# Seven places in the order of work of a four-layer kernel: first turns, bias rows, first logits, passages between layers, masked units, last tiles

## The chip, the cores and the metric

One NeuronCore of a Trainium2 chip runs the whole program. The metric is the time of one execution on the device, in microseconds (us). The engines are named as in the profile: PE (TensorE), DVE (VectorE), ACT (ScalarE), POOL (GpSimd) and SP (SyncE, whose queue issues the DMA transfers). They run their own lists of instructions and meet at semaphores only.

## The reference

The input is x, 2 x 512 tokens of 256 numbers (fp32), eight tiles of 128 tokens. Four layers follow one another, each of the form

```
xn = layernorm(x);  x = x + attn(xn) * silu(ffn(xn))
```

- Layer 0: attention with 16 heads of 128, in which the probabilities are summed over the queries and multiply the values; a mixture of eight experts (256 to 1024 to 256, gelu, a low-rank side path, two experts to a token, 160 slots each) plus a shared expert of the same size.
- Layer 1: an RWKV step (key, value, receptance, and one recurrent state that enters at the first token only); a linear layer.
- Layer 2: attention across the heads' first positions with rotary factors, and eight dense experts (256 to 256) weighted by a gate.
- Layer 3: differential causal attention, 8 heads; a feed-forward network (1024 hidden) with a Walsh-Hadamard transform of the hidden rows.

## The kernel before

Everything stays in on-chip memory; weights are fetched ahead of each stage. Almost every matrix product is made as three products of rounded halves (`product`, lines 101 to 103): an operand is split into a rounded part (ACT or DVE writes it) and the rest (DVE or POOL subtracts). So each stage has the rhythm: PE fills a bank of PSUM, ACT copies it rounded, DVE writes the rest, PE reads both.

Each engine's list is written out by hand, so the order of the statements below is the order of the work.

- **Start.** DVE and POOL normalise the eight tiles of x (`statistics`, `rsqrt`, `normalised`, line 1345), four tiles (batch 0) first. PE turns a tile with `turn_xn` (line 804), ACT copies it (`turned`, line 1941), DVE writes the rest (`turned_rest`, line 1352). Then PE projects head 0: batch 0's first two products, the turns of tiles 4 to 7, then the rest. POOL meanwhile runs `split_qkv(1, ...)` (lines 649 and 652), which splits head 1's weights, and behind it `rest_k(0, ...)` (line 658), the key rests that head 0's scores wait for.
- **Heads.** Sixteen heads, each with eight scores, eight maxima (DVE, line 1394), eight exponentials (ACT, line 1963) and eight accumulations. Head 15 also makes the router's logits: `logits_rows` after score 2, `logits_turn` (line 830) after score 5, which waits for ACT's copy of the logits (line 1972).
- **Experts.** Eight rounds. In a round PE makes nine hidden tiles (`hidden`; tile n needs the bank of tile n - 4 free, which is when DVE has split it, line 1547), turns back the rows of the expert before (`rows_back`), turns the next slots and makes the second product (`rows_of`, which reads split f + 1 for its step f). DVE runs `expert`: for each n a rounding (line 1541) and a rest (line 1547); before n == 2 it runs `rows_biased` (lines 1529 and 1532), which adds the bias to the rows of the expert before. SP stores those rows, loads the bias (line 476), and then, in its next turn, the next slots (lines 486, 487) and the next weights (line 467, 1060 KB). ACT begins to round those weights (line 2023) beside the next expert's hidden tile 0.
- **Shared expert.** `shared_hidden` and `shared_rows` on PE, gelu on ACT (line 2104), `shared_split` on DVE (lines 1580 to 1589). `combine(b)` (line 1611) joins the two experts' rows of a batch; it is called for batch 1 after the residuals of batch 0.
- **Passage from layer 0 to 1.** After the last tile of `shared_rows(1)` PE turns tiles 0 to 3 of the new xn, waits for their rests and projects.
- **Layer 1.** Projections of batch 0 (`rwkv_product`), turns of tiles 4 to 7, four products with a Hadamard matrix (`hadamard`, line 1121) for layer 3's down weights, a wait for ACT's four copies of them (line 2158), projections of batch 1, then `lin_rows` and `out_rows`. DVE: `first_key`, `mixed_values`, `wkv`, then `residuals(1, b)`. ACT: `keys1`, `exponentials1`, `receptance`, then the rounding of layer 2's weights (line 2165), from which POOL subtracts (line 748).
- **Layer 3.** 24 units (g, h, k) of attention: scores, an exponential (line 2301), and, if the unit lies on the diagonal, a mask by POOL (line 791); PE multiplies a unit's probabilities two units later (`values3`, line 1268). Half of the groups have two units, the one off the diagonal first. Then the down product, and `token_major` (line 1070), the output product, with two tiles to a bank; DVE multiplies and adds by pairs (`residual`, lines 1326 and 1329), and SP stores by pairs (line 575).

## Time and profile before

| | |
|---|---|
| median of 3 runs | 888.36 us (887.53 to 889.39) |
| the profiled execution | 889.76 us, of which its span is 888.0 |
| PE busy | 851.4 us (96%) |
| DVE busy | 630.2 us (71%) |
| ACT busy | 465.1 us (52%) |
| POOL busy | 451.2 us (51%) |
| PE's mean granted clock | 0.996 |

Engines work side by side, so busy times don't add up to the span. A granted clock of 1.00 is 2.4 GHz, 0.50 is 1.2 GHz. In a timeline row the first number is the start from the span's beginning, the second the duration; a bracket at its end is the idle time before it and the instruction whose end released it. Products that follow one another overlap in the rows, so the distance of two starts is what one costs. Rows of SPq are the issuing of a transfer, not the transfer.

### The profile page before, as it was taken

How to read it: one execution, taken by the hardware profiler on the slowest of the kernel's cores; microseconds unless marked ns; L12 is line 12 of the kernel's file. 1: busy time of each engine (PE TensorE's matmuls, PEld its weight loads, DVE VectorE, ACT ScalarE, POOL GpSimd, SP SyncE). 2: the span in 40 equal slices, each digit the busy share in tenths (PEclk: the TensorE clock that was granted, in tenths of full speed). 3: DMA queues.
4: the chain of work that ended last, by engine and by line, in shares of the span. 5: the costliest groups of instructions: out<-in, count | busy, mean ns of one | idle time of the engine just before them, and what ended most of it. 6: DMA issues, size and time to landing. Idle time of an engine off the chain costs nothing.

```text
span 888.0 us, 15400 instructions
## 1 busy us (share of the span) xinstructions
PE 851.4 (96%) x5344; PEld 708.8 (80%) x5344; DVE 630.2 (71%) x1255; ACT 465.1 (52%) x928; POOL 451.2 (51%) x299
## 2 busy tenths in 40 slices
PE   5999999999999999999999999899999999989998
PEld 4888888888856899999999878678788887866677
DVE  7798989898987756645656867576677575348655
ACT  2666666666654566655642384633343343256632
POOL 5576767676624555665655003069626227426620
PEclk9999999999999999999999999999999999999999
DMA  8101010101007276465113050011110010000001
GB/s 324 37 19 35 18 35 18 35 18 36 0 0 264 84 256 200 148 205 178 53 35 122 3 201 1 1 49 48 35 59 24 1 60 1 1 1 2 3 1 48
DMA packets 22142, 59.02 MB, mean 66 GB/s; under 512 B 2896, under 2 KB 13392, under 8 KB 19024
## 3 DMA queue, kind: packets, MB, share of 16 engines
q1 hardware_dynamic: 20560, 54.20, 18.4%
q0 software_dynamic: 1536, 4.20, 1.4%
q8 instruction: 30, 0.49, 0.2%
q14 instruction: 16, 0.13, 0.0%
HBM read 50.00 MB, written 8.39 MB: 66 GB/s over the span
## 4 chain that ended last, share of the span: by engine, by line
PE 85%; DVE 7%; ACT 4%; issue 2%; DMA 1%; POOL 1%; POOLq 0%; SPq 0%; DVEq 0%; ACTq 0%
PE banks L101 25%; PE banks L102 24%; PE banks L103 24%; PE banks L1268 3%; PE banks L1255 2%; PE banks L1070 2%; PE banks L940 1%; DVE banks L1784 1%; DVE arenaB_rounded L1541 1%; DMA arenaD<-in_wexp 1%; DVE arenaC_rounded L1547 1%; PE banks L1110 1%; PE banks L875 1%; PE banks L876 1%; DVE arenaC_rounded L1793 1%
## 5 line engine op out<-in xcount | busy, mean ns | idle before, releaser
L1963 ACT ACTIVATE banks<-banks,small 128x512 f32<-128x512 f32 x128 | 84.9, 663 | 79.7 <-DVE small L1394 79.7
L1394 DVE TENSOR_REDUCE small<-banks 128x1 f32<-128x512 f32 x128 | 86.8, 678 | 10.5 <-PE banks L103 10.5
L101 PE MATMUL banks<-xnT_rounded,arenaD_rounded 128*128 128x512 f32 x224 | 90.8, 405 | 2.9 <-DVE s_tok_rounded L1352 2.9
L102 PE MATMUL banks<-s_tok_rounded,arenaD_rounded 128*128 128x512 f32 x224 | 91.3, 408 | 0.0
L103 PE MATMUL banks<-arenaC_rounded,arenaD_rounded 128*128 128x512 f32 (+1 forms) x256 | 89.6, 350 | 0.0
L103 PE MATMUL banks<-xnT_rounded,arenaC_rounded 128*128 128x512 f32 x192 | 77.5, 403 | 0.0
L103 PE MATMUL banks<-xnT_rounded,arenaD_rounded 128*128 128x512 f32 x192 | 75.9, 395 | 0.0
L101 PE MATMUL banks<-arenaC_rounded 128*128 128x512 f32 (+1 forms) x192 | 71.3, 371 | 2.8 <-DVE arenaC_rounded L1547 2.8
L1409 DVE SCALAR_TENSOR_TENSOR arenaC<-banks,small,arenaC 128x512 f32<-128x512 f32 x96 | 71.2, 741 | 0.0
L102 PE MATMUL banks<-arenaD_rounded,arenaC_rounded 128*128 128x512 f32 (+1 forms) x192 | 68.5, 357 | 0.0
L663 POOL TENSOR_TENSOR arenaD_rounded<-arenaC,ones 128x512 fp32r<-128x512 f32 x30 | 31.3, 1042 | 55.1 <-DVE arenaC L1409 54.1
L101 PE MATMUL banks<-arenaB_rounded,arenaC_rounded 128*128 128x320 f32 (+2 forms) x176 | 57.4, 326 | 0.0
L101 PE MATMUL banks<-xnT_rounded,arenaB_rounded 128*128 128x512 f32 x128 | 52.0, 406 | 3.3 <-DVE arenaC_rounded L1793 1.1
L101 PEld LDWEIGHTS banks<-xnT_rounded,arenaD_rounded 128*128 128x128 f32 x224 | 43.4, 194 | 13.9 <-POOL arenaC_rounded L677 1.9
L103 PEld LDWEIGHTS banks<-arenaC_rounded,arenaD_rounded 128*128 128x128 f32 x256 | 48.0, 188 | 5.5
L102 PEld LDWEIGHTS banks<-s_tok_rounded,arenaD_rounded 128*128 128x128 f32 x224 | 43.3, 193 | 9.9
L709 POOL TENSOR_TENSOR arenaD_rounded<-arenaD,arenaB_rounded 128x1024 fp32r<-128x1024 f32 (+1 forms) x12 | 37.5, 3140 | 26.8 <-ACT arenaB_rounded L2023 26.8
L658 POOL TENSOR_TENSOR arenaD_rounded<-arenaD,arenaC_rounded 128x512 fp32r<-128x512 f32 x32 | 41.4, 1294 | 17.8 <-ACT arenaD L1954 17.8
L2209 ACT ACTIVATE arenaC<-banks 128x512 f32<-128x512 f32 x32 | 18.9, 599 | 59.5 <-PE banks L103 59.5
L1784 DVE TENSOR_TENSOR banks<-banks,arenaC 128x512 f32<-128x512 f32 x32 | 22.4, 700 | 36.7 <-PE banks L103 32.3
L103 PE MATMUL banks<-arenaB_rounded,arenaC_rounded 128*128 128x256 f32 (+1 forms) x144 | 47.7, 331 | 0.0
L102 PE MATMUL banks<-arenaB_rounded,arenaC_rounded 128*128 128x320 f32 (+2 forms) x144 | 47.3, 329 | 0.0
(408 smaller groups left out, 2634.5 us busy)
## 6 DMA issues: line engine op xcount, KB each, us to landing
arenaD<-in_wexp SPq DMA_DIRECT2D x8, 1060.0 KB, 6.6
arenaD<-in_wexp SPq DMA_DIRECT2D x8, 1024.0 KB, 4.9
arenaC<-in_wqkv SPq DMA_DIRECT2D x16, 384.0 KB, 3.1
arenaD<-in_wexp SPq DMA_DIRECT2D x8, 512.0 KB, 3.6
slots<-arenaB SPq DMA_DIRECT2D x1, 2560.0 KB, 10.3
arenaB<-in_sw SPq DMA_DIRECT2D x1, 2084.0 KB, 7.4
arenaC<-in_wo SPq DMA_DIRECT2D x1, 2048.0 KB, 14.9
arenaC<-slots SPq DMA_DIRECT2D x8, 256.0 KB, 2.8
```

The costliest lines, as they stand in the source:

```text
L101: pe.matmul(o, r(lhs[0]), r(rhs[0]), start=start, stop=False)
L102: pe.matmul(o, r(lhs[0]), r(rhs[1]), start=False, stop=False)
L103: return pe.matmul(o, r(lhs[1]), r(rhs[0]), start=False, stop=stop)
L658: pool.tensor_tensor(r(klo[q][:, sl]), klo[q][:, sl], rounded(kT[q][:, sl]), ALU.subtract).then_inc(klo_done, 1)
L663: pool.tensor_tensor(r(acc_hi[b]), acc[b], ones[:, 0:1].to_broadcast([P, S]), ALU.mult).then_inc(acc_rounded, 1)
L709: pool.tensor_tensor(r(v), v, rounded(h), ALU.subtract).then_inc(w_split, 1)
L1268: mm = pe.matmul(bank[6 + m % 2][32 * hh:32 * hh + 32, 256 * which + q0 - 256 * h:256 * which + 256], lhs, prob3[u % 4][:, hh, at:at + w], ...
L1394: dve.tensor_reduce(negmax[:, n % 4:n % 4 + 1], bank[3 + n % 4][:, :], AX.X, ALU.max, negate=True).then_inc(max_done, 1)
L1409: ins = dve.scalar_tensor_tensor(acc[n // ST], prob[n % 4], inv, acc[n // ST], ALU.mult, ALU.add)
L1784: dve.tensor_tensor(v, v, gs[n % 2], ALU.mult).then_inc(gu_done, 1)
L1963: act.activation(prob[r], prob[r], ACT.Exp, bias=negmax[:, r:r + 1], accum_out=rowsum[:, r:r + 1]).then_inc(exp_done, 1)
L2209: act.activation(gs[n % 2], bank[n % 2][:, :], ACT.Silu).then_inc(silu2_done, 1)
```

## The change

Seven places; nothing is computed otherwise.

1. First turns: PE runs twelve products of a matrix of ones into an unused bank before its first turns; POOL waits for all eight normalised tiles before it splits head 1's weights.
2. First logits: `logits_turn` is called after score 7 and not after score 5.
3. Expert bias rows: `rows_biased` is called before hidden tile 6 and not before tile 2.
4. Passage from layer 0 to 1: tiles 0 to 3 are turned ahead of the last tile of `shared_rows(1)`; the eight operations of `combine(1)` go in between the steps of `shared_split(1, ...)`.
5. Layer 1 and the passage to layer 2: two of the four Hadamard products and their copies move behind the turns of layer 2's tiles 4 to 7; ACT rounds layer 2's weights before `keys1(1)` and not after `receptance(1)`; tiles 0 to 3 are turned ahead of the last tile of `out_rows`.
6. Masked units first: a group's unit on the diagonal comes before the one off it.
7. Last tiles: the last two tiles are multiplied, added and stored one by one, the last from a bank of its own.

```diff
-        UNITS3 = [(g, h, k) for g in range(8) for h in range(2) for k in range(0, 2 * h + 2, 2)]
+        UNITS3 = [(g, h, k) for g in range(8) for h in range(2) for k in range(2 * h, -2, -2)]
         DIAGONAL3 = [n for n, (g, h, k) in enumerate(UNITS3) if k == 2 * h]
...
+        WARM_UP = 12
...
-            for i in range(NT // 2):
+            for i in range(NT // 2 - 1):
                 sp.wait_ge(x_done, (layers - 1) * NT // 2 + i + 1)
                 sp.dma_start(out[256 * i:256 * i + 256, :].rearrange("(n p) d -> p n d", p=P), x[:, 2 * i:2 * i + 2, :]).then_inc(x_out, 16)
-            sp.wait_ge(x_out, 16 * NT // 2)
+            for t in (NT - 2, NT - 1):
+                sp.wait_ge(x_done, layers * NT // 2 + t - NT + 2)
+                sp.dma_start(out[P * t:P * t + P, :], x[:, t, :]).then_inc(x_out, 16)
+            sp.wait_ge(x_out, 16 * (NT // 2 + 1))
...
             rsqrt(0, (2, 3))
+            pool.wait_ge(xn_done, NT)
             split_qkv(1, 1, 0)
             rest_k(0, 0, 0)
             rest_k(0, 0, 1)
...
+            pe.wait_ge(filled, ONES)
+            for n in range(WARM_UP):
+                pe.matmul(bank[7][:, 0:P], ones[:, :], ones[:, :], start=True, stop=True)
             turn_xn(0, range(NT // 2))
...
                     if last and n == 2:
                         pe.wait_ge(v_done, 2 * NH)
                         logits_rows()
-                    if last and n == 5:
-                        logits_turn()
                     if n == 7:
+                        if last:
+                            logits_turn()
                         colsum(h, 0, whole=last)
...
             def shared_rows(b):
                 for t in range(ST * b, ST * b + ST):
+                    if t == NT - 1 and layers > 1:
+                        turn_xn(1, range(ST))
                     o = bank[4 + t // 2][:, (t % 2) * D:(t % 2 + 1) * D]
...
-                def hadamard():
-
-                    pe.wait_ge(wff3_in, 16)
-                    pe.wait_ge(kr_done, 2)
-                    for i in range(4):
-                        if i >= 2:
-                            pe.wait_ge(had_copied, i - 1)
-                        pe.matmul(bank[i % 2][:, :], con[:, C_HAD:C_HAD + P], w_down3[:, 2 * i:2 * i + 2, :].rearrange("p f d -> p (f d)"),
+                HAD_BANK = (0, 1, 6, 7)
+
+                def hadamard(parts):
+
+                    for i in parts:
+                        pe.matmul(bank[HAD_BANK[i]][:, :], con[:, C_HAD:C_HAD + P], w_down3[:, 2 * i:2 * i + 2, :].rearrange("p f d -> p (f d)"),
                                   start=True, stop=True).then_inc(had_ready, 1)
 
-                turn_xn(1, range(ST))
                 pe.wait_ge(fold_split, 7)
                 turned(1, 1)
                 rwkv_product(0, 0, (0, 1))
...
                 turn_xn(1, range(ST, NT))
                 if layers > 2:
-                    hadamard()
-                    pe.wait_ge(had_copied, 4)
+                    pe.wait_ge(wff3_in, 16)
+                    pe.wait_ge(kr_done, 2)
+                    hadamard((0, 1))
+                    pe.wait_ge(had_copied, 2)
                 turned(1, 3)
                 pe.wait_ge(kr_done, 2)
                 rwkv_product(0, 1, (0, 1))
...
                 pe.wait_ge(rwkv_done, 2)
                 for t in range(ST, NT):
+                    if t == NT - 1 and layers > 2:
+                        turn_xn(2, range(ST))
                     out_rows(t)
                 if layers > 2:
-                    turn_xn(2, range(ST))
                     pe.wait_ge(wq_split, 1)
                     qkv_rows(w_qkv2, w_qkv2_hi, 2, range(ST))
             if layers > 2:
 
                 turn_xn(2, range(ST, NT))
+                hadamard((2, 3))
                 qkv_rows(w_qkv2, w_qkv2_hi, 2, range(ST, NT))
+                pe.wait_ge(had_copied, 4)
                 pe.wait_ge(qkv_done, 2 * NT)
...
@@ -1267,7 +1279,7 @@
                             lhs = ones[:, 0:32] if which else v3[:, ST * b + kt, 32 * head:32 * head + 32]
                             mm = pe.matmul(bank[6 + m % 2][32 * hh:32 * hh + 32, 256 * which + q0 - 256 * h:256 * which + 256],
                                            lhs, prob3[u % 4][:, hh, at:at + w],
-                                           start=(kt == 0), stop=(kt == 2 * h + 1), tile_position=(0, 32 * hh))
+                                           start=(kt == 2 * h), stop=(kt == 1), tile_position=(0, 32 * hh))
                     return mm
...
-                    if k == 0 and m >= 2:
+                    if u == GROUPS3[m][0] and m >= 2:
                         pe.wait_ge(norm3_done, m - 1)
                     mix3(m, u, 0)
...
                 pe.wait_ge(wgo3_in, 32)
                 pe.wait_ge(norm3_done, 16)
-                token_major(yT3, w_out3, 4, s_ready)
+                token_major(yT3, w_out3, 4, s_ready, range(NT - 1))
+                pe.wait_ge(ffn_done, NT)
+                for c in range(DC):
+                    mm = pe.matmul(bank[3][:, 0:D], yT3[:, c, (NT - 1) * P:NT * P], w_out3[:, c, :], start=(c == 0), stop=(c == DC - 1))
+                mm.then_inc(s_ready, 1)
...
             def expert(e, q, back=None, last=False):
                 for n in range(NF + 2):
 
-                    if n == 2 and back is not None:
+                    if n == 6 and back is not None:
                         rows_biased(*back)
                     if n <= NF:
                         dve.wait_ge(hid_done, HID0 + 9 * e + n + 1)
@@ -1602,15 +1618,17 @@
...
-            def combine(b):
-
-                dve.wait_ge(rows_got[b], 16 * 2 * ST)
-                dve.wait_ge(bias_done, 3)
-                for k in range(2):
-                    for t in range(ST * b, ST * b + ST):
-                        ins = dve.scalar_tensor_tensor(got[0][:, t, :], got[k][:, t, :], wt[:, t, k:k + 1], got[0][:, t, :] if k else sb2,
-                                                       ALU.mult, ALU.add)
-                    link(ins)
+            def combine(b, parts=range(2 * ST)):
+
+                for j in parts:
+                    if j == 0:
+                        dve.wait_ge(rows_got[b], 16 * 2 * ST)
+                        dve.wait_ge(bias_done, 3)
+                    k, t = j // ST, ST * b + j % ST
+                    ins = dve.scalar_tensor_tensor(got[0][:, t, :], got[k][:, t, :], wt[:, t, k:k + 1], got[0][:, t, :] if k else sb2,
+                                                   ALU.mult, ALU.add)
+                    if j % ST == ST - 1:
+                        link(ins)
...
             combine(0)
             shared_sum(0)
             shared_sum(1)
-            shared_split(1, range(2, NF + 1))
+            for f, parts in zip(range(2, NF + 1), ((), (0, 1), (2, 3), (4,), (5,), (6,), (7,))):
+                shared_split(1, (f,))
+                combine(1, parts)
...
             residuals(0, 0)
-            combine(1)
             rests(1, 0)
             shared_sum(2)
             shared_sum(3)
...
-                between(3)
+                for i in range(NT // 2 - 1):
+                    residual(3, i)
+                dve.wait_ge(silu_done, NT // 2 * 4)
+                for t, o in ((NT - 2, bank[7][:, 0:D]), (NT - 1, bank[3][:, 0:D])):
+                    dve.wait_ge(s_ready, NT * 3 + t + 1)
+                    g = g_tok[:, t, :]
+                    link(dve.scalar_tensor_tensor(g, o, 1.0 - LAMBDA_INIT, g, ALU.mult, ALU.mult))
+                    dve.tensor_tensor(x[:, t, :], x[:, t, :], g, ALU.add).then_inc(x_done, 1)
...
@@ -2152,17 +2178,21 @@
                 keys1(0)
                 exponentials1(0)
                 turned(1, (2, 3))
+
+                def hadamard_copy(i, b0):
+                    act.wait_ge(had_ready, i + 1)
+                    act.copy(had_b[:, 2 * i:2 * i + 2, :].rearrange("p f d -> p (f d)"), bank[b0][:, :]).then_inc(had_copied, 1)
+
                 if layers > 2:
-                    for i in range(4):
-                        act.wait_ge(had_ready, i + 1)
-                        act.copy(had_b[:, 2 * i:2 * i + 2, :].rearrange("p f d -> p (f d)"), bank[i % 2][:, :]).then_inc(had_copied, 1)
+                    hadamard_copy(0, 0)
+                    hadamard_copy(1, 1)
                 receptance(0)
+                if layers > 2:
+                    act.wait_ge(w2_in, 16)
+                    act.copy(r(part(arenaC, 10752, DC * (768 + E2))), part(arenaC, 0, DC * (768 + E2))).then_inc(wq_rounded, 1)
                 keys1(1)
                 exponentials1(1)
                 receptance(1)
-                if layers > 2:
-                    act.wait_ge(w2_in, 16)
-                    act.copy(r(part(arenaC, 10752, DC * (768 + E2))), part(arenaC, 0, DC * (768 + E2))).then_inc(wq_rounded, 1)
                 gate_silu(1)
                 turned(2, (0, 1))
...
                 round_gateup(0, 0, 0)
                 qkv_copy(2, 2, 4)
                 turned(2, (2, 3))
+                hadamard_copy(2, 6)
+                hadamard_copy(3, 7)
                 round_gateup(1, 1, 0)
                 qkv_copy(2, 4, 6)
                 round_down(0, 0, 0)
```

## Rows read from the trace of the kernel before

**Rows 1.** The page, chain that ended last, share of the span by engine.

```profile
PE 85%; DVE 7%; ACT 4%; issue 2%; DMA 1%; POOL 1%; POOLq 0%; SPq 0%; DVEq 0%; ACTq 0%
```

**Rows 2.** PE's waits, whole span: us in total, times, longest.

```profile
PE banks L101 <- DVE s_tok_rounded L1352: 7.1, 5, 1.7
PE banks L804 <- DVE xn L1345: 7.0, 2, 6.5
PE banks L101 <- DVE arenaC_rounded L1547: 5.2, 8, 1.1
...
PE banks L830 <- ACT arenaC L1972: 1.8, 1, 1.8
PE banks L1268 <- POOL arenaB L791: 1.5, 1, 1.5
```

**Rows 3.** Timeline, 6 to 19 us: start, duration, engine and line.

```profile
6.94 0.73 DVE L1345 TENSOR_SCALAR xn<-x,meanvar,rstd 128x256 f32<-128x256 f32 x2 [0.27 <-POOL rstd L593]
...
12.99 1.46 POOL L649 TENSOR_TENSOR arenaD_rounded<-arenaC,ones 128x768 fp32r<-128x768 f32 x1
...
13.06 3.44 DVE L1345 TENSOR_SCALAR xn<-x,meanvar,rstd 128x256 f32<-128x256 f32 x2 [0.27 <-POOL rstd L593]
...
18.39 0.66 PE L101 MATMUL banks<-xnT_rounded,arenaD_rounded 128*128 128x512 f32 x1 [1.40 <-DVE s_tok_rounded L1352]
```

**Rows 4.** Stretches of 1 us: busy time (x instructions) by engine, granted clock, DMA.

```profile
14.00:15.00 1.00, 1.00 (x4) 0.81 (x3) 1.00 (x2) 0.00 (x0) 0.92 (x2) 1.00 1.09 471
...
19.00:20.00 1.00, 1.00 (x4) 0.81 (x3) 0.03 (x1) 0.27 (x1) 0.65 (x1) 0.50 1.11 475
...
22.00:23.00 1.00, 1.00 (x6) 0.81 (x5) 0.85 (x4) 0.00 (x0) 0.00 (x0) 1.00 0.00 0
```

**Rows 5.** Timeline, PE, the four Hadamard products.

```profile
517.78 3.68 PE L1121 MATMUL banks<-arenaD,con 128*128 128x512 f32 x8
```

**Rows 6.** Timeline, DVE, last head's seventh row maximum.

```profile
260.23 0.69 DVE L1394 TENSOR_REDUCE small<-banks 128x1 f32<-128x512 f32 x1
```

**Rows 7.** Timeline, one round of the expert loop (DVE, PE, SP queue, ACT).

```profile
334.25 0.69 DVE L1529 TENSOR_TENSOR arenaC<-banks,arenaD 128x512 f32<-128x512 f32 x1
334.97 0.43 DVE L1532 TENSOR_TENSOR arenaC<-banks,arenaD 64x256 f32<-64x256 f32 x1
...
336.50 0.41 PE L101 MATMUL banks<-arenaC_rounded,arenaB_rounded 128*128 128x320 f32 x1 [0.67 <-DVE arenaC_rounded L1547]
...
336.96 0.40 SPq L476 DMA_DIRECT2D arenaD<-in_b  x1
...
342.18 0.33 SPq L467 DMA_DIRECT2D arenaD<-in_wexp  x1
...
349.55 0.61 ACT L2023 CAST arenaB_rounded<-arenaD 128x512 fp32r<-128x512 f32 x1
```

**Rows 8.** DMA issues of the expert weights: the loop's six, then the slowest.

```profile
arenaD<-in_wexp SPq DMA_DIRECT2D x6, 1060.0 KB, 6.6
...
arenaD<-in_wexp SPq DMA_DIRECT2D x1, 1060.0 KB, 7.5
```

**Rows 9.** Timeline around the end of layer 0 (PE, DVE).

```profile
492.02 0.43 DVE L1580 CAST arenaC_rounded<-arenaB 128x512 fp32r<-128x512 f32 x1 [0.38 <-ACT arenaB L2104]
...
496.74 0.39 PE L1051 MATMUL banks<-xn_rounded,arenaB_rounded 128*128 128x256 f32 x1
...
503.55 1.67 DVE L1611 SCALAR_TENSOR_TENSOR arenaC<-arenaC,small,arenaB 128x256 f32<-128x256 f32 x4
```

**Rows 10.** Timeline around layer 1 (PE, POOL, DVE).

```profile
522.14 0.50 PE L101 MATMUL banks<-xnT_rounded,arenaC_rounded 128*128 128x512 f32 x1 [0.68 <-ACT arenaB L2158]
...
533.79 4.06 POOL L748 TENSOR_TENSOR arenaC_rounded<-arenaC,arenaC_rounded 128x1552 fp32r<-128x1552 f32 x1 [17.35 <-ACT arenaC_rounded L2165]
...
536.63 1.77 DVE L1329 TENSOR_TENSOR x<-x,g_tok 128x512 f32<-128x512 f32 x1
```

**Rows 11.** Timeline, DVE, the last pair of tiles.

```profile
883.99 0.69 DVE L1326 SCALAR_TENSOR_TENSOR g_tok<-banks,g_tok 128x512 f32<-128x512 f32 x1 [0.31 <-PE banks L1070]
```

## Prediction

> **What bounds the kernel now.** I read the chain of work that ended last first: TensorE (PE) holds 85% of it, VectorE (DVE) 7%, ScalarE (ACT) 4% [rows 1]. So an edit is worth what it takes out of PE's idle time or slow clock, and nothing else. The second view is PE's own waits: 7.1 us in five stalls for the rests of the turned activations, 7.0 us for the normalised rows (6.5 of it the kernel's start), 5.2 us in eight stalls in the experts, 1.8 us for the logits, 1.5 us for the last causal mask, and others of 2.0 us or less that no edit names [rows 2]. The third is the order of time around each edit, the fourth the granted clock.
>
> The profiled execution took 889.76 us, 1.76 outside its span of 888.0; the runs' median is 888.36. I take the gain off the profiled one and carry it to the median.
>
> **First turns.** POOL's work on head 1's weights begins at 12.99, and beside it two normalisations of the tokens take 3.44 us, where the same pair alone took 0.73 [rows 3]. The new wait holds that work (the 1.46 us rounding and the subtraction behind it) until the eighth tile. The pair then ends at 13.79 and not 16.50: 2.7 us. The held work, 3.3 us long, ends near 17.2; its readers are head 1's first projection (after 21) and, behind it in POOL's queue, head 0's first key rest, which started at 19.35. Both are later, so the wait costs nothing. From the end of the pair to the first projection of batch 1 ran 18.39 - 16.50 = 1.9 us [rows 3]: it would start at 15.7.
>
> That needs PE free by 13.8. It is not at today's pace: the twelve projections from 10.01 start four to the microsecond until 14.84 [rows 4]. At 1.2 GHz (granted 0.50) four start, at 2.4 GHz six in one with overlap: 0.43 against 0.235 us each [rows 4]. The twelve warm-up products are 128 columns of fp32. Four of 512 columns took 3.68 us [rows 5], so one of 128 costs 0.22 at 2.4 GHz and 0.44 at 1.2: 2.6 to 5.3 us. PE stands idle for the first 6.5 us [rows 2] and its companions start work at 1.6, so they end about when the first turn may start; at worst 0.4 after, which the turns' own wait for rows hides. Today the dense stretch from 18.39 brings the clock from 0.50 back to 1.00 by 22 [rows 4]; the warm-up is as dense, so I expect the fast pace at 10.0. The twelve projections are then through at 12.9, and batch 1's 24 run at 0.235, where today eight ran at 0.43 (19 to 22 [rows 4]): 1.5 us more. All together 4.1. But by 19 it was at 0.50, after PE had mostly waited from 16 to 18.4, and the new order keeps gaps of some 1.5 us before 10.0 and before 15.7. If the warm-up bought nothing, the twelve end at 14.85, the turns at 16, batch 1 starts at 17.8: 0.6. Bounds 0.6 and 4.1; I take 3.4, near the top, because more work lies ahead of both gaps than today.
>
> The Trainium skill, "TensorE: Matmul & The Clock Gate", section "What's actually happening", says that the number of slow products at a kernel's start varies between executions of the same kernel. By it this term would come in some runs and not in others, 4.1 or down to 0.6; the trace of one execution can't show that.
>
> **First logits.** The eight small turns move from after score 5 to after score 7. PE's 1.8 us wait [rows 2] goes, but scores 6 and 7 need banks that DVE frees, and DVE's maximum of score 6 at 260.23 [rows 6] has no wait in front: it was DVE that came late, not the score. Head 15's end is DVE and ACT in turn. Worth 0.1; bounds 0 and 0.3. Their reader, at 267, is not touched.
>
> **Expert bias rows.** Two additions, 0.69 and 0.43 us, sit on DVE before hidden tile 2's rounding, and PE then waits 0.67 for the split of tile 1 [rows 7]. Without them it ends 0.8 earlier, ahead of the 335.83 at which PE wants it. At tile 6 they lie behind split 4, the last that a hidden tile waits for; splits 5 to 8 come 1.1 us later (split 8 near 342.3), and the second product reads split 8 at 343.1. The first of the eight stalls (1.1) has no bias rows before it: 5.2 - 1.1 = 4.1 over seven.
> What becomes late is SP. It waits for the additions before it stores the rows and loads the bias, and behind these stand the next slots and the next 1060 KB. The additions end near 339.3; today the bias load goes out 1.56 us after they end (335.40 to 336.96 [rows 7]), and two slot loads and the branch put another 1.7 before the big one: near 342.6 instead of 342.18 [rows 7]. It lands after 6.6 us as the median of six, 7.5 at the worst [rows 8]: 349.2 to 350.1. ACT rounds from it at 349.55 [rows 7], in the new order 0.67 earlier, at 348.9. Late by 0.3 to 1.2, of which the round soaks up 0.45: today 1.12 us of additions cost PE only 0.67. I take 0.1 a round, 3.5, since half of the six land sooner than that median. Bounds 1.0 (0.5 a round) and 4.1.
>
> **Passage 0 to 1.** Today PE waits 1.7 after the four turns, the longest of the five stalls [rows 2]. The turns now stand before the last shared tile, whose 2.9 us cover copy and rest. But the second combination moves into the split loop: eight operations of 0.42 us, 3.3 in all, between splits with 0.38 us of idle time in front of each [rows 9], so DVE leaves the loop 1.25 us later (five such gaps of about 0.4 are all it can use). The matmul at 496.74 already waits for the last split (it shows 0.39 us, its like 0.28 [rows 9]) and passes on 0.85 of it; the normalised rows come 1.25 later, so the turns end at 505.1 and the last tile at 508.05. Gain 0.4; bounds 0 and 1.7.
>
> **Passage 1 to 2.** Of the four Hadamard products (3.68 us [rows 5]) two move behind the later turn, into one of the five stalls; with them goes the 0.68 us wait for the last copy [rows 10]. PE reaches the next projections at about 519.95, not 522.14 [rows 10]: 2.2 with the 0.4. Then the chain through DVE decides. The rounding of the next layer's weights moves before the second batch's keys: ACT ends it near 524.0 and POOL subtracts for 4.06 us [rows 10], 524 to 528.1. In that stretch DVE does the first key's small steps and batch 0's products, all with both inputs in SBUF. The nearest row is an addition of that kind, which took 1.77 for 0.69 and ended 0.5 after POOL's subtraction, begun at 533.79 [rows 10]. So the first key waits to 528.1, exponentials and gates follow it, and batch 0's residual starts near 535.9, where it is today. What is left is the 1.08 that the residual no longer loses to POOL: rows normalised 1.0 earlier. The turn put before the last output tile hides 1.2 of PE's next wait. PE starts the projections near 544.0 instead of 546.18; the two Hadamard products behind the next turn (1.75 against a stall of 1.4) give back 0.2. For both passages together 2.0; bounds 0.4 (only the first) and 3.1 (DVE not held up).
>
> The Trainium skill, "SBUF — State Buffer", section "Who interferes with whom", speaks against this move: a DVE instruction with two SBUF inputs is shut out for the whole of a GpSimd instruction that reads SBUF. By it the small steps wait out all of the 4.06 us and the sum is my 2.0; without it, 2.7.
>
> **Masked units first.** PE's last wait is 1.5 us for the mask of the very last unit [rows 2], with 0.1 more before it. Now the last unit has no mask, and its neighbours' mask ends under the last scores. Inside the loop two masks still follow each other, and PE has no gap. 1.6; bounds 0.8 and 1.9.
>
> **Last tiles.** The last pair's product starts on DVE at 883.99, after 0.31 us of waiting, takes 0.69 [rows 11], and an addition as long follows: 885.4. In the new order tile 6 can't start before the third residual ends, at 883.7, and four half-size operations of 0.42 [rows 9] with the waits between them take 1.75: 885.4 again. Only the last store is half as large. 0.1; bounds 0 and 0.6 (half of the last pair's two operations).
>
> **Sum.** 3.4 + 0.1 + 3.5 + 2.0 + 1.6 + 0.1 = 10.7 us. 889.76 - 10.7 = 879.1 profiled, 888.36 - 10.7 = 877.7 as median. All upper bounds (4.1, 0.3, 4.1, 3.1, 1.9, 0.6) make 14.1: 874.3. All lower ones (0.6, 0, 1.0, 0.4, 0.8, 0) 2.8: 885.6.
>
> **Rivals.**
> The clock does not hold: the fast pace is lost in a gap and the first term is 0.6, the sum 7.9: 880.5. For it: the clock fell once in this stretch. Against: PE is idle for less of it now. 0.20.
> The expert loads become the bound: landings of 7 us and more together with the stores give 0.5 a round: 880.2. For it: the median landing is already at the limit. Against: the 0.45 of slack. 0.13.
> A passage gives nothing: DVE's backlog of combinations or POOL's subtraction reaches PE, 2.0 becomes 0.4: 879.3. 0.12.
> Slower: SP's queue in the experts. If each of six loads came 2.0 us later than I place it, the loop would lose what all else gains: (10.7 + 1.8) / 6 = 2.1 a round decides for slower by over 0.2%. It needs landings over 9 us. 0.04.
> No change: the gains lie on PE but some other engine holds the same pace, within 1.8 us of 888.36. The 851 us for which PE was busy speak against it. 0.04.
> The forecast: 0.47.
>
> **Numbers.** 0.2% (1.8 us) is what a measurement of this kernel tells from no change. All cases but the last two are faster: 0.92; 0.04 within; 0.04 slower. For 8 in 10 I go from 874.3 to 883.0: above it lie half of the cases in which two rivals meet, no change and slower.
>
> **What would show it.** Right: the pair of normalisations near 0.8 us; six products a microsecond from 10; no wait on split rows in experts 1 to 7; PE's projections of layer 2 two microseconds sooner after the experts; no wait for a mask at the end. Wrong: granted clock 0.50 between 15 and 20; ACT idle before the first rounding of a round for a DMA; DVE's first-key steps of 0.16 us stretched to over 2 with PE waiting behind them; a wait on the last output tile's turn of over 2 us.

## The result

The changed kernel takes 882.98 us (median of 5 runs, 880.82 to 883.76) against 888.36 for the kernel before, a ratio of 0.9923 with an interval of 0.9908 to 0.9939. That is faster by 5.4 us, half of the 10.7 forecast, and inside the predicted range (874.3 to 883.0) by 0.02 us only: 877.7 was forecast. The profiled executions stand at 889.76 and 883.27, 6.5 us apart; the table below goes by them. Each entry is what PE gains in us between two marks that both kernels have; the times are those of the changed kernel. (The same product of the last head starts at 250.00 before and at 245.45 after, so 4.55 us are gained by then.)

| stretch | forecast | trace |
|---|---|---|
| start to the last head (245.45) | 3.4 | 4.55 |
| to the first expert's stall (313.31) | 0.1 | 0.09 |
| experts (to 445.94) | 3.5 | 1.49 |
| offset products and shared expert (to 489.35) | 0 | -1.62 |
| both passages (to 549.66) | 2.0 | 3.16 |
| layer 2 and the start of layer 3 (to 780.73) | 0 | -0.08 |
| attention of layer 3 (to 847.55) | 1.6 | -1.49 |
| end | 0.1 | 0.43 |
| sum | 10.7 | 6.53 |

The first turns, the passages and the end came out higher than forecast, the experts and the attention lower, and one loss stands where no edit is. The waits of PE in the changed kernel, beside those of before [rows 2]:

```profile
PE banks L101 <- DVE arenaC_rounded L1563: 3.2, 5, 1.1
PE banks L1267 <- ACT arenaC L2333: 2.4, 5, 0.9
PE banks L101 <- DVE s_tok_rounded L1368: 1.4, 1, 1.4
PE banks L809 <- DVE xn L1361: 1.3, 3, 0.8
```

The three s_tok stalls between the layers are gone (1.72, 1.05 and 1.46 us before), and so is the wait for the last mask; of the two at the start one is left, and the other stands under POOL's subtraction now (1.6 us). The experts' stalls fell from eight to five and not to one. The second row, which counts one of the two buffers only, holds a wait for an exponential that comes back in the loop of layer 3's attention.

**Start** (timeline of DVE, POOL and PE, beside [rows 3]; then two windows beside [rows 4], whose columns are the same):

```profile
12.77 0.74 DVE L1361 TENSOR_SCALAR xn<-x,meanvar,rstd 128x256 f32<-128x256 f32 x2 [0.26 <-POOL rstd L597]
13.58 1.47 POOL L653 TENSOR_TENSOR arenaD_rounded<-arenaC,ones 128x768 fp32r<-128x768 f32 x1 [0.85 <-DVE xn L1361]
15.40 0.50 PE L101 MATMUL banks<-xnT_rounded,arenaD_rounded 128*128 128x512 f32 x1 [1.40 <-DVE s_tok_rounded L1368]
```
```profile
17.00:18.00 1.00, 1.00 (x6) 0.82 (x5) 0.27 (x1) 0.60 (x1) 1.00 (x1) 1.00 0.84 360
19.00:20.00 1.00, 1.00 (x6) 0.81 (x5) 0.00 (x0) 0.68 (x3) 0.35 (x1) 1.00 0.96 410
```

The pair of normalisations took 0.74 us where it took 3.44. Batch 1's projections start 3.0 us earlier, six to the microsecond from the first, and that pace brings the other 1.55 of the 4.55.

**Experts** (timeline of the SP queue, ACT and PE, the round of [rows 7]; the DMA issues beside [rows 8]):

```profile
336.31 0.40 SPq L477 DMA_DIRECT2D arenaD<-in_b  x1
338.52 0.33 SPq L468 DMA_DIRECT2D arenaD<-in_wexp  x1
```
```profile
339.94 2.19 ACT L2049 CAST arenaC_rounded<-arenaD 128x512 fp32r<-128x512 f32 x4 [3.82 <-DMA arenaD<-in_b]
345.45 0.62 ACT L2049 CAST arenaB_rounded<-arenaD 128x512 fp32r<-128x512 f32 x1 [1.22 <-DMA arenaD<-in_wexp]
```
```profile
347.57 0.41 PE L101 MATMUL banks<-arenaC_rounded 128*128 128x320 f32 x1 [0.50 <-DVE arenaC_rounded L1563]
...
arenaD<-in_wexp SPq DMA_DIRECT2D x6, 1060.0 KB, 7.1
```

Read it from the bottom. PE waits 0.50 for the split of tile 1. ACT hands out tile 1 only after its first rounding, and this waited 1.22 for the 1060 KB load. That load went out at 338.52, behind the stores and the bias load, and took 6.9. Before, it went out at 342.18; with the 4.63 us gained so far, 338.52 stands for 343.15, so it is 1.0 late in its round. In every round in which ACT waits for this load PE stalls two microseconds later (347.57, 365.13, 382.64, 416.99, by 0.48 to 0.58; by the distance to before's products each costs 0.64 to 0.74); in the other two it doesn't. ACT's wait of 3.8 for the bias load is another thing that the prediction did not see: the second group of roundings counts the bias load too.

**Clock after the experts and in layer 3's attention** (windows):

```profile
448.00:449.00 1.00, 1.00 (x7) 1.00 (x8) 0.00 (x0) 0.00 (x0) 0.00 (x0) 0.57 0.00 0
451.00:452.00 1.00, 1.00 (x4) 0.74 (x3) 0.90 (x5) 0.00 (x0) 0.00 (x0) 0.50 0.00 0
455.00:456.00 1.00, 1.00 (x6) 0.82 (x5) 0.00 (x0) 0.62 (x2) 0.75 (x1) 1.00 0.00 0
783.00:784.00 1.00, 1.00 (x16) 0.78 (x11) 0.00 (x0) 0.21 (x1) 0.72 (x1) 0.50 0.00 0
788.00:789.00 1.00, 1.00 (x20) 0.74 (x16) 1.00 (x1) 1.00 (x2) 0.17 (x1) 0.50 0.00 0
```

The kernel before fell to 0.50 (1.2 GHz) from 455.5 to 458.9, the changed one from 448.1 to 455.0. The offset products lost 0.35 by that (2.95 against 2.60 us), the turns of the last rows 0.6 (1.2 against 0.6), the first products of the shared expert 0.7: the 1.6 of the table. In the attention the kernel before kept 1.00 throughout; the changed kernel was at 0.50 from 782.6 to 789.5.

**The loop of layer 3's attention** (timeline of PE: before, then the changed kernel):

```profile
803.01 0.94 PE L1255 MATMUL banks<-g_tok,s_tok 32*128 32x256 f32 x16
...
799.35 0.94 PE L1267 MATMUL banks<-g_tok,s_tok 32*128 32x256 f32 x16 [0.20 <-ACT arenaB L2333]
```

The scores of a unit follow without a gap before, and wait 0.20 us for an exponential in the changed kernel. That wait comes once in every three units, six times in all.

**Passage 1 to 2** (timeline of POOL, DVE and PE, beside [rows 10]):

```profile
515.42 0.50 PE L101 MATMUL banks<-xnT_rounded,arenaC_rounded 128*128 128x512 f32 x1 [0.68 <-ACT arenaB L2184]
...
519.47 3.55 POOL L753 TENSOR_TENSOR arenaC_rounded<-arenaC,arenaC_rounded 128x1552 fp32r<-128x1552 f32 x1 [7.96 <-ACT arenaC_rounded L2192]
...
520.90 2.13 DVE L1740 TENSOR_TENSOR small<-small 128x2 f32<-128x2 f32 x1 [4.18 <-ACT small L2160]
...
538.62 0.47 PE L101 MATMUL banks<-arenaC_rounded,xnT_rounded 128*128 128x512 f32 x1
```

A step of two columns that takes 0.16 us took 2.13 and ended with POOL's subtraction. The wait of 0.68 for the last Hadamard copy is still there, behind two copies as behind four.

### The profile page after: what moved, and what is told of

Its sections match the earlier page's. It is cut to its first block, busy times and chain, and to the rows that moved or that the text cites. A ratio compares the mean times of both kernels' runs of the same rounds, so it can differ in the third digit from the quotient of the medians.

```text
span 881.4 us, 15452 instructions
## 1 busy us (share of the span) xinstructions
PE 857.4 (97%) x5368; PEld 712.3 (81%) x5368; DVE 625.3 (71%) x1257; ACT 465.3 (53%) x928; POOL 448.9 (51%) x299
## 4 chain that ended last, share of the span: by engine, by line
PE 83%; DVE 6%; DMA 4%; ACT 3%; issue 2%; SPq 1%; POOL 0%; DVEq 0%; ACTq 0%; POOLq 0%
PE banks L101 23%; PE banks L102 22%; PE banks L103 22%; PE banks L1280 4%; DMA arenaD<-in_wexp 3%; PE banks L1267 3%; PE banks L1080 1%; DVE banks L1803 1%; PE banks L948 1%; PE banks L1120 1%; PE banks L883 1%; PE banks L884 1%; DVE arenaC_rounded L1812 1%; PE banks L809 1%; DMA arenaC<-in_wqkv 1%
## 5 line engine op out<-in xcount | busy, mean ns | idle before, releaser
L101 PE MATMUL banks<-arenaB_rounded,arenaC_rounded 128*128 128x320 f32 (+2 forms) x176 | 57.4, 326 | 0.0
L597 POOL TENSOR_TENSOR rstd<-veps,mhalf 128x2 f32<-128x2 f32 x16 | 12.2, 761 | 72.7 <-DVE veps L1356 72.7
```

Of the source, the lines that this page charges most:

```text
L101: pe.matmul(o, r(lhs[0]), r(rhs[0]), start=start, stop=False)
```

## The experiments

Each kernel ran in 5 rounds against the kernel before on its own chip. The median of before was 890.04 us for the first four, 891.68 for the next four and 890.61 for the last four, so kernels are compared by their ratio to it. 0.001 of ratio is 0.9 us.

### Units in the old order: units_back

```
-UNITS3 = [... for k in range(2 * h, -2, -2)]
+UNITS3 = [... for k in range(0, 2 * h + 2, 2)]
```

The blocks that open and close a group's accumulation go back with it.

> The kernel after, with the units of layer 3's attention back in the old order (unmasked first). The changed kernel's trace has a wait of 0.20 us for an exponential once in each group and a period of 7.81 us a group where before had 7.60; it also has 6.9 us at granted clock 0.50 at the start of this attention. Theory A (the order itself costs 0.2 us a group, and its gain at the end, 1.5 us, only pays that back; the slow clock there is chance): the period is 7.60 again, PE waits 1.5 us for the last mask again, and the time is that of the changed kernel within 1 us, 881 to 883. Theory B (the new order also brings the clock down at the start): the clock stays at 1.00 there in this kernel and it is 1.5 us faster than the changed kernel. Theory C (the new order is worth the 1.6 us of the forecast): 1.5 us slower than the changed kernel, with the period unchanged.

0.9912 (0.9889 to 0.9935). The attention (from its first scores' start to the end of its last products) took 66.24 us, with the old wait of 1.49 at its end and no wait in the loop, and the clock fell at 784 here too. Theory B falls: the fall comes with the old order as well. A holds, C doesn't.

### Bias rows back: bias_back

```
-if n == 6 and back is not None:
+if n == 2 and back is not None:
```

> The kernel after, with the bias rows of the experts back at hidden tile 2. The changed kernel still has four stalls of 0.5 us for the split of tile 1, each behind a wait of ScalarE of 1.2 us for the next expert's first load. Theory A (the loads, issued 1.0 us later in their round than before, took most of this part's gain): seven stalls of 0.57 to 0.67 us come back, none of them with a wait for a load, and the kernel is slower than the changed one by 1.5 us only. Theory B (the forecast, 0.5 us a round): slower by 3.5 us.

0.9901 (0.9884 to 0.9918), no slower than the changed kernel. Seven stalls of 0.57 to 0.60 came back, and no ACT wait for a load. From the first rank product of the rows (the one that closes each half of an expert's second product) to the last it took 125.1 us, as before did, and the changed kernel 123.6. The same stretch, with the bias rows of the change, took 122.4 to 124.4 in no_warm, units_end and fill, and 125.1 to 127.7 in round_back, units_back and no_hold, where one load came so late that PE stalled for 1.8 to 2.7 us; in units_back and no_hold the clock fell behind it. The median of the seven traces is 124.4. So this part is worth about 0.7 us, in some executions nothing. The trace is A's (seven stalls, no wait for a load); that the whole runs aren't slower, neither theory had.

### Loads ahead of the stores: loads_first, stores_late

```
 for e in range(NE - 2):
     sp.wait_ge(hid_done, HID0 + 9 * e + 9)
     load_slots(e + 2, e % 2)
     load_first(e + 2, e % 2)
+    if e:
+        store_rows(e - 1, 1 - e % 2)
+        load_bias(e + 1, 1 - e % 2)
     sp.wait_ge(y_ready, 4 * e + 2)
     load_second(e + 2, e % 2)
-    store_rows(e, q)
-    load_bias(e + 2, q)
...
```

That is loads_first; in stores_late the added lines stand behind load_second. In both, two more things change: the loop is written out instead of run as a loop, and the bias load counts on the semaphore of the stores, so that ACT's second roundings don't wait for it. No run takes the three apart.

> The kernel after, with the DMA queue's order in the experts changed: the next slots and the first 1060 KB go out before the rows are stored and the bias is loaded, and the bias load is counted by another semaphore, so that ScalarE's second group of roundings doesn't wait for it. Theory A (the late first load causes the four stalls): the load goes out 2 us or more earlier, ScalarE doesn't wait for it, no stall is left but the first, and the kernel is 2 us faster than the changed one. Theory B (the stalls come from DVE's own queue of splits): ScalarE's wait goes, the stalls of 0.5 us stay, and the time is that of the changed kernel.

0.9864 (0.9839 to 0.9888), some 5 us faster than the changed kernel. The stretch accounts for 1.0 of it: it fell to 122.6 us. This execution also had no fall of the clock behind the experts and a shorter one in the attention, but one at the start. Two stalls were left besides the first, 0.54 and 0.93, each behind an ACT wait for the first load, which now landed after 8.4 us as the median.

> The kernel after, with the DMA queue's order in the experts changed once more: slots and first load, then the second load of the same expert, and only behind it the stores of the rows and the bias load, which is counted by another semaphore. With the loads ahead of the stores the first load went out earlier but took 8.4 us as its median instead of 7.1, and two of six rounds still stalled. Theory A (the stores and the bias load beside the first load lengthen it): the first load lands after 6.6 us or less as the median, ScalarE doesn't wait for it, no round but the first stalls, the stretch from the first rank product of the rows to the last takes 121.5 to 122.5 us (changed kernel 123.6, before 125.1), and the kernel is 2 us faster than the changed one. Theory B (the length of the landing has to do with something else, such as the slots): still 7 us and more, stalls in some rounds, stretch 122.7 or longer.

0.9860 (0.9833 to 0.9886). The stretch took 120.3 us, less than A expected, and the waits hold one stall in place of five. That is 3.3 us less than in the changed kernel; the whole runs are some 5.6 faster, and what the rest is no trace shows. SP queue, then PE's waits:

```profile
336.34 0.43 SPq L468 DMA_DIRECT2D arenaD<-in_wexp  x1
...
343.73 0.43 SPq L520 DMA_DIRECT2D rows<-arenaC  x1
```
```profile
PE banks L101 <- DVE arenaC_rounded L1564: 1.1, 1, 1.1
```

The load goes out 2.2 us sooner, lands after 6.9 as the median (the trace has the landing of three of the six), and ACT waits for none. 125.1 - 120.3 = 4.8 us: the bias rows' whole gain, 4.1 by the forecast's upper bound, was there, and the queue of loads had withheld it. Before had no ACT wait for a load, so its stalls were the bias rows'; the new queue with the bias rows at their old place was not run.

### Single-column products among the last rows: offs_spread

```
-rows_of(NE - 1, NE // 2 - 1, 1)
+rows_of(NE - 1, NE // 2 - 1, 1, offset_products)
```

In the second half of these rows, offset_products puts two of the twelve products behind each hidden tile's product from the second on; the block of twelve behind the rows is gone.

> The kernel after, with the twelve offset products of one column (24 passes in 3.1 us) moved from behind the last expert to places between the products of its last rows. In both traces the granted clock falls to 0.50 some 2 to 3 us after these begin, and stays there 3.4 us before and 6.5 us after. Theory A (the sparse stretch brings the clock down): the clock stays at 1.00 after the experts; PE waits 0.8 us for the copy of the last rows, which the products hid, and 2 to 3 us are gained all the same against the changed kernel. Theory B (the fall is due to the long dense stretch before, or to chance): the fall comes all the same, and the kernel is 0 to 0.5 us slower or faster.

0.9908 (0.9892 to 0.9923). The clock stayed at 1.00 after the experts. But it did so too in units_back, loads_first and no_warm, with the products at the old place. From the last rank product but one to the shared expert's first product it took 7.86 us (with 0.58 of waiting for the copy), against 7.02 in units_back and 7.94 in the changed kernel, whose clock had fallen and whose next products lost 0.7 more: the move costs 0.8 where the clock holds. The stretch of the experts, which holds the moved products here, took 129.0 us with a stall of 2.17 and a fall of the clock behind it. Open: whether the sparse stretch brings the fall.

### Masked first only at the end: units_end

```
-for k in range(2 * h, -2, -2)
+for k in ((2, 0) if g == 7 and h else range(0, 2 * h + 2, 2))
```

The accumulation's opening and closing blocks follow.

> The kernel after, with the masked unit first only in the very last of the sixteen groups of layer 3's attention, and unmasked first in all others. Theory A (0.2 us a group is the price of the order in the loop, 1.5 us its gain in the last group alone): the period is 7.60 us, no wait for an exponential in the loop, no wait for the last mask, and the kernel is 1.2 to 1.4 us faster than the changed one. Theory B (the two belong together): the wait at the end stays in some form, and the kernel is no faster than the one with all units back, within 0.5 us.

0.9902 (0.9875 to 0.9929). No wait at the end, none in the loop but at its start: A, as a structure. The clock was at 0.50 from 784 to 791, and the attention took 65.55 us with it, 1.3 less than the changed kernel.

### Filler behind the first scores: fill

```
 scores3(u)
+if u < 2:
+    for i in range(4):
+        pe.matmul(bank[7][:, 0:P], ones[:, :], ones[:, :], start=True, stop=True)
```

> The kernel after, with four more products of 128 columns, whose result nobody reads, behind each of the first two scores of layer 3's attention, where PE waits 0.9 us for an exponential. The changed kernel, the one with its units back and two others all show granted clock 0.50 for 3 to 7 us from there; before shows none. Theory A (the pauses of 0.9 us bring the clock down): it stays at 1.00 there, and the kernel is 1.5 us faster than the changed one. Theory B (the fall comes from something else, such as the small products of a quarter of the rows): the clock falls all the same, and the kernel is the same within 0.5 us or slower by what the products delay the scores.

0.9902 (0.9874 to 0.9931). The clock stayed at 1.00 and the attention took 65.0 us (changed kernel 66.9). The run's own time doesn't show this apart from noise.

### No warm-up: no_warm

```
-for n in range(WARM_UP):
-    pe.matmul(bank[7][:, 0:P], ones[:, :], ones[:, :], start=True, stop=True)
```

> The kernel after, without the twelve warm-up products at the start. Theory A (they set the pace of the first projections): the granted clock is 0.50 from 10 to 15 us, four products a microsecond, batch 1's projections start near 16.9 instead of 15.4, at 0.50 for 3 us more, and all that follows is 3 us later: 3 us slower than the changed kernel. Theory B (the wait of POOL gave most of the 4.6 us): 1 us slower or less.

0.9921 (0.9895 to 0.9946): as fast as the changed kernel, where A had 3 us slower. The profiled execution shows no fall of the clock behind its start, and its six runs had a mean granted clock of 0.998, the changed kernel's 0.994. Start (PE, timeline; windows):

```profile
18.09 0.50 PE L101 MATMUL banks<-xnT_rounded,arenaD_rounded 128*128 128x512 f32 x1 [1.56 <-DVE s_tok_rounded L1365]
```
```profile
13.00:14.00 1.00, 1.00 (x4) 0.80 (x3) 0.73 (x3) 0.00 (x0) 0.23 (x1) 1.00 0.95 410
19.00:20.00 1.00, 1.00 (x6) 0.81 (x5) 0.00 (x0) 0.20 (x1) 1.00 (x1) 1.00 0.99 426
```

Batch 1 started 2.7 us later than in the changed kernel, at 18.09 where A had 16.9: A for the start, and not for the whole run. The clock's column says 1.00 at 13, yet four products start in the microsecond: at the start the count of products tells the pace and the column doesn't. The attention, masked first and without a fall, took 64.9 us: 0.5 less than before.

### No hold on POOL: no_hold

```
-pool.wait_ge(xn_done, NT)
```

> The kernel after, without POOL's wait for the eighth normalised tile ahead of head 1's weights. Theory A (the forecast: POOL's work beside the normalisations costs 2.7 us): a pair of normalisations takes over 3 us again instead of 0.7, the later turns wait for it, and batch 1's projections start 2 us or more later than 15.4. Theory B (without warm-up products the wait brought only 0.3 us to the start of batch 1): it is worth 0.3 us, because the projections of batch 0, which stand ahead of the turns on PE, hide it; with the fast pace they no longer do, so it lies between 0.3 and 2.7: a start near 17 to 18 us.

0.9954 (0.9941 to 0.9968), 2.8 us slower than the changed kernel (part of this can be the clock: its six runs had a mean granted clock of 0.992, the changed kernel's 0.994). DVE's pair and batch 1's start:

```profile
13.00 3.43 DVE L1360 TENSOR_SCALAR xn<-x,meanvar,rstd 128x256 f32<-128x256 f32 x2 [0.26 <-POOL rstd L597]
...
18.33 0.79 PE L101 MATMUL banks<-xnT_rounded,arenaD_rounded 128*128 128x512 f32 x1 [1.40 <-DVE s_tok_rounded L1367]
```

A: 2.9 us at batch 1. By these traces warm-up and hold are worth 2.7 and 2.9 us, each with the other there; together 3.0 at this mark. Neither brings much alone, since both must be there for the turns to come early. The price of the warm-up is one pair of traces, though: with both edits batch 1 started anywhere from 15.33 to 18.72 in ten traces, and without the warm-up at 18.09 and, in best_no_warm, at 16.83.

### Rounding back behind the second receptance: round_back

```
 receptance(0)
-act.copy(r(part(arenaC, 10752, DC * (768 + E2))), part(arenaC, 0, DC * (768 + E2))).then_inc(wq_rounded, 1)
 keys1(1)
 exponentials1(1)
 receptance(1)
+act.copy(r(part(arenaC, 10752, DC * (768 + E2))), part(arenaC, 0, DC * (768 + E2))).then_inc(wq_rounded, 1)
```

> The kernel after, with the rounding of layer 2's weights back behind the second batch's receptance. In the changed trace POOL's subtraction (519.47 to 523.02) holds VectorE's first small step of the first key from 520.90 to 523.03 (0.16 us of work), as forecast, and yet layer 2's projections start 3.1 us sooner than the earlier gains explain, not 2.0. Theory A (VectorE's chain sets the end, and each us of such holding costs one): the small steps take 0.16 us, the subtraction comes beside the residuals and holds those up instead by 1.1 us, and the projections start 0.5 to 1 us sooner than in the changed kernel. Theory B (the move is worth what I took for it, 1.1 us): they start 0.5 to 1.1 us later.

0.9937 (0.9924 to 0.9951); its clock fell at 9.7 to 16.5 us as well. From layer 1's first projection to layer 2's it took 34.94 us, the changed kernel 34.97, before 37.70. The small step took 0.16 us, and the residual's addition beside POOL 1.77 (0.69 alone). DVE, timeline:

```profile
532.49 0.69 DVE L1344 TENSOR_TENSOR g_tok<-g_tok,banks 128x512 f32<-128x512 f32 x1 [1.40 <-PE banks L1120]
533.21 1.77 DVE L1345 TENSOR_TENSOR x<-x,g_tok 128x512 f32<-128x512 f32 x1
```

Both theories miss: where POOL's 4 us lie doesn't matter here.

### The best of them: best, best_no_warm

The kernel after with stores_late, units_end and fill; the second without the warm-up.

> The kernel after with three edits tried one by one before: the loads of the experts ahead of the stores and the bias load, the masked unit first only in the very last group of layer 3's attention, and the filler products behind its first two scores. Alone, the first took the rank products' stretch from 123.6 to 120.3 us; with the second the attention takes 65.6 us with a fall of the clock in it and should take 63.9 without; with the third the clock stayed at 1.00 there. Theory A (each is worth what its own trace shows): no stall in the experts but the first, attention 63.6 to 64.0 us at granted clock 1.00, and 3.3 + 3.0 = 6 us faster than the changed kernel, 1.5 to 2.5 us faster than the one with the loads alone. Theory B (the clock falls there by chance, whatever stands in the pauses): 65.5 us for the attention, and 1.3 us faster than the one with the loads alone.

0.9838 (0.9825 to 0.9852): 876.16 us against 890.61, 14.5 us faster than before and some 7.6 faster than the changed kernel. Attention (timeline, PE):

```profile
776.11 0.94 PE L1272 MATMUL banks<-g_tok,s_tok 32*128 32x256 f32 x16 [0.88 <-DVE arenaB L1912]
776.97 1.16 PE L1257 MATMUL banks<-ones 128*128 128x128 f32 x8
778.06 1.15 PE L1272 MATMUL banks<-g_tok,s_tok 32*128 32x256 f32 x16
779.14 1.16 PE L1257 MATMUL banks<-ones 128*128 128x128 f32 x8
780.34 0.94 PE L1272 MATMUL banks<-g_tok,s_tok 32*128 32x256 f32 x16
```

63.8 us at granted clock 1.00, as A had it; the rank products' stretch 120.4.

> The same kernel without the twelve warm-up products. Without them the changed kernel was as fast as with them, though everything from the heads on stood 2.7 us later, and its mean granted clock was 0.998 instead of 0.994. Theory A (falls of the clock are chance, and that one had fewer): the mean clocks of the runs are those of the kernel with them, and it is 1.5 to 2.7 us slower. Theory B (more dense work early brings later falls): its mean clock is higher by 0.003 again, and the two are equal within 0.5 us.

0.9859 (0.9844 to 0.9874), 2.5 us slower, mean clocks 0.997 to 0.998 against 0.995 to 1.000: A. Later falls of the clock are no fewer without the warm-up. The attention took 63.8 here too, at 1.00. But the two traces stand 3.9 us apart, and the start is 1.3 of that. The other 2.5 lie in the rows of the shared expert:

```profile
472.83 0.28 PE L103 MATMUL banks<-arenaD_rounded,arenaB_rounded 128*128 128x256 f32 x1 [0.66 <-issue]
...
474.26 0.38 PE L102 MATMUL banks<-arenaB_rounded,arenaD_rounded 128*128 128x256 f32 x1 [0.68 <-issue]
```

PE pauses here for nothing that the profile shows. Such pauses stand at this place in six of the fourteen traces (stores_late, units_end, fill, no_warm, no_hold and this one), and their cause is open. So the 2.5 us of the medians aren't shown to be the warm-up's alone.

## Why the prediction was right, and where its steps failed

The number came out inside the range by luck in part: three terms missed upwards by 2.6 us together, the experts and the loop of the attention downwards by 3.2, and the clock, which no term held behind the start, took 3.5 more; the median run then gained 1.1 less than the profiled one. Two of the prediction's signs of being wrong stood in the trace, ACT idle for a DMA before a round's first rounding, and a first-key step stretched to over 2 us, though PE didn't wait behind it.

**First turns: the mechanism right, 4.55 for 3.4.** The hold, the fast pace from about 10 and the clock that stays were as forecast; the term passed its upper bound (4.1, though the forecast's own 2.7 and 1.5 make 4.2), because batch 1 started at 15.4 and not 15.7. The rival that the clock doesn't hold was no phantom: in the traces of fill, bias_back, loads_first, round_back and no_hold, five of the eleven with the warm-up, it fell to 0.50 between 9.7 and 12 us, and batch 1 of fill started at 16.90 instead of 15.40, that of round_back at 18.72. That fits what the Trainium skill says under "TensorE: Matmul & The Clock Gate", section "What's actually happening": that the number of slow products at the start varies between executions. The changed kernel's trace is among the six that kept the pace. Over the ten traces with both edits, the hundredth product behind batch 1's first starts on average 3.6 us ahead of the one in before's only trace, close to the 3.4.

**Expert bias rows: the step that failed.** "It lands after 6.6 us as the median ... Late by 0.3 to 1.2, of which the round soaks up 0.45 ... I take 0.1 a round, 3.5." The load was issued 1.0 late in its round, not 0.4, since from the bias load to it passed 2.2 us and not 1.7, and it landed after 7.1 as the median. Four of six rounds lost 0.7 each and the term was 1.5. This is the rival that the expert loads become the bound. It had a chance of 0.13; its price, 0.5 for each of six rounds, is near the 2.6 that were lost in all. Over all executions even 1.5 is on the good side. That it is the queue of loads, and not DVE's splits, is shown by stores_late: splits and bias rows unchanged, loads first, 4.8 us instead of 1.5.

**Masked units first: the mechanism at the end was right, the loop was not.** "Inside the loop two masks still follow each other, and PE has no gap." It has one: 0.20 us for an exponential, once in three units, six times. The period of three units is 7.81 us instead of 7.60 (DVE's reciprocals at 802.87 and 818.49, two periods apart, against 816.04 and 831.24). What stands between two scores decides. The values of an unmasked unit take 1.07 us, those of a masked one 0.86; the masked one now lies in the slot in which PE is ahead of ACT, and 0.21 is missing. 1.6 at the end less six waits of 0.20 in the loop leaves 0.4; no_warm and fill measure 0.5 and 0.4 (64.9 and 65.0 against 65.4). units_end and best, with the order only where it pays, show the forecast's 1.6: 65.4 - 63.8. The other 2.0 us of this row are the clock.

**The clock, which no term held.** The attention begins with PE pausing three times for about 0.9 us. Of eleven traces without filler, before's among them, nine read 0.50 somewhere in the 8 us behind it and two don't (before, no_warm); of three with filler none does. That the filler helps is likely and not proven. The fall in units_back shows that it doesn't need the new order of units. What the falls cost in whole runs can be estimated: over all runs here a kernel's time rises by about 0.6 us for each 0.001 that its mean granted clock is lower. The changed kernel's five runs had 0.994, before's on three chips 0.996; that is 1.2 us of what is missing.

**Passages: 3.2 for 2.0, just over the upper bound, by another way than the bound's.** DVE was held up as forecast (2.13 us for a step of 0.16, till POOL's end), as the Trainium skill has it under "SBUF — State Buffer", section "Who interferes with whom". The step that failed came behind: "batch 0's residual starts near 535.9, where it is today". It started at 530.45, which is 535.0 with the 4.5 gained ahead of the passages added back. POOL's subtraction took 3.55 us and not 4.06 and ended at 527.5 in that count, not 528.1, and DVE's steps behind it took 7.4 and not 7.8, so PE found the rows ready and waited no more before layer 2's projections. One more step failed without harm: the 0.68 us wait for the last Hadamard copy was to go and stayed, but the forecast's 2.2 at these projections had not counted it, and 2.2 is what the trace has. The forecast priced a DVE that isn't held up twice, at 3.1 and at 2.7; no run shows either. round_back shows that the sum doesn't hang on POOL's place at all: the early place costs 2.0 on the small step, the late one 1.1 on the residual and 1.4 of waiting for PE, and PE's projections start at the same distance.

**First logits 0.09 for 0.1, last tiles 0.4 for 0.1.** The first is as forecast: PE's 1.8 us wait is gone, and it waits for DVE instead, 0.52 before the eighth score and 0.47 behind it. The second was mis-sized. DVE's last operation ended 2.1 us before the span did, not 2.6: the half-size store lands sooner, while the four half-size operations took what the pair had, as the prediction said.

**No change, slower:** nothing came of them.

## What to carry to other kernels

When work is moved out of a compute engine's way, follow it into the DMA queue behind it: here the order of the issues in that queue, with the bias load's semaphore and the written-out loop that changed along with it, decided over 3.3 of 4.8 us, and it could be read from ACT's wait for a DMA two microseconds before each stall of PE. A reordering that repairs the last step of a loop belongs into the last step alone; in the loop, count what lies between two waits, because the same work in another slot can cost something each time round. And where kernels differ by some 5 us and the clock falls in several places by chance, compare stretches between marks at equal clock before an edit is blamed or praised.

## What the runs showed of the hardware

The granted clock of a sequence of the same instructions differs between executions: behind the experts it fell in before (3.4 us), after (6.8) and eight others, and not in four; no_warm's profiled execution shows none, no_hold's had five. A fall came also inside a dense loop, at 350 to 356 us in units_back, offs_spread and no_hold, each time behind a single stall of 1.8 to 2.7 us (behind one of 1.9 in round_back it did not). And the 1060 KB load took 8.4 us as its median with 320 KB of stores and the bias load right behind it, against 6.9 with these out of its way (three landings); the 256 KB store took 6.4 there instead of 2.2.
